# A transposing DMA for the attention operands, and three steps moved in the slots around it

## The reference

```
def expmap0(v): n = |v|;  return tanh(n) * v / n
def logmap0(x): n = |x|;  return arctanh(min(n, 1 - 1e-5)) * x / n
def plin(x, w, b): return expmap0(logmap0(x) @ w + b)
...
ada = t_emb @ w_ada + b_ada          # six rows of 256 for each sequence
xn = layer_norm(logmap0(x))
xm = expmap0(xn * (1 + sc_msa) + sh_msa)
q = _to_heads(plin(xm, w_q, b_q))    # 16 heads of 16; k and v alike
...
scores = einsum('bhqd,bhkd->bhqk', qt, kt) / sqrt(16)
attn = softmax(scores)
out_h = expmap0(einsum('bhqk,bhkd->bhqd', attn, vt))
attn_out = plin(_from_heads(out_h), w_o, b_o)
x = mobius_add(residual, expmap0(g_msa * logmap0(attn_out)))
...                                  # then an MLP half in the same manner
```

## Time and profile before

| | us |
|---|---|
| median of 3 runs | 839.33 (838.67 to 840.11) |
| the profiled execution | 841.73 |
| its span on the core | 839.9 |
| prologue, up to the first projection | 61.6 |
| attention half, first to last projection | 61.6 to 530.8 |

### The profile page before, as it was taken

One profiled execution on the slowest core, in us unless ns is written; L12 is line 12 of the kernel. 1 busy time (PEld: TensorE's weight loads), 2 busy tenths in 40 slices (PEclk: granted clock), 3 DMA queues, 4 the chain that ended last, 5 costly groups with the idle time before them and its releaser, 6 DMA issues.

```text
span 839.9 us, 29703 instructions
## 1 busy us (share of the span) xinstructions
PE 703.7 (84%) x9393; PEld 515.0 (61%) x9393; DVE 673.6 (80%) x2231; ACT 586.5 (70%) x1627; POOL 353.3 (42%) x682
## 2 busy tenths in 40 slices
PE   5967999999999999999999999731868899889986
PEld 2756777777777777777777777520325555556555
DVE  3868888888888888888888888757797888888885
ACT  1125777777777777777777777633577888888874
POOL 1005555556555565555555565401232333233231
PEclk9979999999999999999999999955899999999999
DMA  9931111111111111111111110021343545455432
GB/s 324 354 86 52 51 52 51 56 56 46 50 54 56 56 43 51 56 56 52 44 54 56 55 46 27 23 66 51 88 116 98 148 137 144 126 150 151 138 102 100
DMA packets 51811, 73.99 MB, mean 88 GB/s; under 512 B 7081, under 2 KB 34609, under 8 KB 51762
## 3 DMA queue, kind: packets, MB, share of 16 engines
q1 hardware_dynamic: 49970, 70.55, 28.4%
q10 hardware_dynamic: 1792, 2.89, 0.9%
HBM read 64.24 MB, written 9.18 MB: 87 GB/s over the span
## 4 chain that ended last, share of the span: by engine, by line
PE 44%; DVE 25%; issue 14%; DMA 5%; ACT 4%; SPq 3%; DVEq 2%; POOL 2%; POOLq 0%; ACTq 0%
PE p_qkv L893 21%; PE p_oz L867 8%; DVE u L1156 7%; PE p_s L958 3%; PE p_s L883 3%; DMA mod_b<-mod_rows 3%; SPq L365 2%; DVE g_all L1191 2%; PE p_qkv L958 2%; PE p_oz L861 2%; DMA x_all<-in_x 2%; DVEq L50 2%; PE p_t L944 1%; DVE qk L1231 1%; PE p_o L972 1%
## 5 line engine op out<-in xcount | busy, mean ns | idle before, releaser
L893 PE MATMUL p_qkv<-wqkv,tT 128*128 128x256 f32 x768 | 194.3, 390 | 26.6 <-DVE u L1156 26.3
L893 PEld LDWEIGHTS p_qkv<-wqkv,tT 128*128 128x128 f32 x768 | 135.1, 192 | 57.4 <-issue 23.8
L477 POOL TENSOR_TENSOR qk<-qk 128x512 f16<-128x512 f32 x64 | 73.9, 1155 | 142.0 <-ACT qk L613 142.0
L907 PEld LDWEIGHTS p_o<-v,pT 64*64 64x64 f32 x4096 | 68.3, 136 | 36.1 <-issue 36.1
L1184 DVE TENSOR_TENSOR z<-p_oz,bo 128x256 f32<-128x256 f32 x64 | 27.1, 424 | 77.5 <-PE p_oz L867 77.3
L618 ACT ACTIVATE qkT<-p_s 128x1024 f32<-128x1024 f32 x64 | 65.5, 1023 | 31.1 <-PE p_s L850 31.1
L907 PE MATMUL p_o<-v,pT 64*64 64x17 f32 x4096 | 72.8, 209 | 12.0 <-ACT pT L663 12.0
L663 ACT ACTIVATE pT<-p_s 128x1024 f32<-128x1024 f32 x64 | 65.4, 1022 | 20.3 <-PE p_s L883 20.3
L867 PE MATMUL p_oz<-wo,oT 128*128 128x256 f32 x256 | 75.2, 418 | 0.6 <-ACT oT L623 0.5
L850 PE MATMUL p_s<-ident,qk 128*128 128x128 f16 x1024 | 67.9, 219 | 6.7 <-issue 4.5
L1222 DVE TENSOR_TENSOR qk<-u,fac 128x256 f32<-128x256 f32 x128 | 70.3, 588 | 0.1
(11 more groups left out here) (268 smaller groups left out, 1758.0 us busy)
## 6 DMA issues: line engine op xcount, KB each, us to landing
mod<-mod_rows SPq DMA_DIRECT2D x128, 128.0 KB, 2.8
x_all<-in_x SPq DMA_DIRECT2D x8, 1024.0 KB, 13.9
gate<-mod_rows SPq DMA_DIRECT2D x128, 64.0 KB, 2.5
mod<-mod_rows SPq DMA_DIRECT2D x32, 256.0 KB, 4.1
mod_b<-mod_rows SPq DMA_DIRECT2D x32, 256.0 KB, 4.1
out<-x_all SPq DMA_DIRECT2D x32, 256.0 KB, 2.2
gate<-gate_rows SPq DMA_DIRECT2D x32, 128.0 KB, 3.5
bqkv<-gate_rows SPq DMA_DIRECT2D x32, 128.0 KB, 3.8
```

What stands on the lines that cost most here:

```text
L477: pool.tensor_tensor(low, qk[:, :].rearrange("p (a h d) -> p a h d", a=2, d=HD), qk4[:, :, :, 0, :], ALU.subtract).then_inc(low_ready, 1)
L893: mm = pe.matmul(p_qkv[:, a * D:a * D + D], tT[:, k, c, :], wqkv[:, c, a * D:a * D + D], start=c == 0, stop=c == C - 1)
L907: mm = pe.matmul(p_o[S * e:S * e + S, col:col + VW], pT[keys, e, g, :], v[keys, k, 2 * g + e, :], start=True, stop=True, skip_group_check= ...
```

## The change

The 16 matmul transposes and the copy out of PSUM are gone. In their place SP issues one DMA with transpose=True for each tile, from qk4 in SBUF to qkT in SBUF. qk4 gets a second buffer by parity (qk4s), which lies over mod_b, a tensor of the second half; bias_left, which had lain there, moves to xa. scores waits for the DMA's semaphore qkT_in instead of the copy's, and also for the exponential that last read p_s.

A new lag L_G = 7 holds gate_z, dot_x, the square of the gated z, and keep_stats; the sums st are double. So there is one slot more, 71 in place of 70. SP fetches the gate rows at lag 6 instead of 5. ScalarE makes the high parts ahead of the output copy evac_oT. GpSimd makes the low parts behind the token root. VectorE's order behind the row sums is gate, clip, dot, repeats, bias sum; it was bias sum, repeats, gate, clip, dot.

```diff
@@ sync
                 if on(h, off, L_H):
                     i, k = 2 * h + off - L_H, (off - L_H) % 2
+                    sp.wait_ge(again_ready, 2 * i + 2)
+                    after(sp, s_psum, i)
+                    sp.sem_inc(rows_begun, 1)
+                    sp.dma_start(qkT[:, :, :, :].rearrange("p a g n -> p (a g) n"),
+                                 qk4s[k].rearrange("p a h r d -> p (a h r d)"), transpose=True).then_inc(qkT_in, 16)
+                if on(h, off, L_L):
+                    i, k = 2 * h + off - L_L, (off - L_L) % 2
                     after(sp, zg_ready, i - 1)
                     for b in range(TB):
                         sp.dma_start(gate[S * b:S * b + S, k, :], mod_row(i, b, 2 * D, 3 * D)).then_inc(gate_in[k], 16)
@@ scalar
-            def high_parts(i):
+            def high_parts(i, k):
 
                 act.wait_ge(qk_ready, 2 * i + 2)
-                after(act, qkT_psum, i)
-                after(act, low_ready, i)
-                after(act, again_ready, 2 * i)
-                act.activation(qk4[:, :, :, 0, :], qk[:, :].rearrange("p (a h d) -> p a h d", a=2, d=HD), ACT.Copy).then_inc(high_ready, 1)
-
-            def evac_qkT(i):
-                act.wait_ge(qkT_psum, i + 1)
-                after(act, s_psum, i)
-                act.activation(qkT[:, :, :, :].rearrange("p a g n -> p (a g n)").bitcast(F32), p_s[:, :], ACT.Copy).then_inc(qkT_ready, 1)
+                after(act, qkT_in, 16 * (i - 1))
+                act.activation(qk4s[k][:, :, :, 0, :], qk[:, :].rearrange("p (a h d) -> p a h d", a=2, d=HD), ACT.Copy).then_inc(high_ready, 1)
@@ tensor
             def scores_wait(i):
 
-                pe.wait_ge(qkT_ready, i + 1)
+                pe.wait_ge(qkT_in, 16 * i + 16)
+                after(pe, p_ready, i)
...
-                if on(h, off, L_H):
-                    transpose_qk(2 * h + off - L_H)
```

More of the change, by code:

```diff
@@ L325, in run_tiles @@
         def run_tiles(eng, slot):
-            run_slots(eng, slot, FIRST, T, T + L_L)
+            run_slots(eng, slot, FIRST, T, T + L_G)
         def run_pairs(eng, slot):
@@ L469, in scale_v, with low_parts, keep_stats @@
                                    fac[:, 2 * H:3 * H].unsqueeze(2).broadcast_to([P, H, HD]), ALU.mult).then_inc(v_ready, 1)
-            def low_parts(i):
+            def low_parts(i, k):
                 pool.wait_ge(high_ready, i + 1)
                 pool.wait_ge(qk_ready, 2 * i + 2)
-                after(pool, qkT_psum, i)
-                low = bass.AP(qk4[:, :, :, :, :].tensor, 2 * HD, [[8 * H * HD, P], [4 * H * HD - HD, 2], [4 * HD, H], [1, HD]])
-                pool.tensor_tensor(low, qk[:, :].rearrange("p (a h d) -> p a h d", a=2, d=HD), qk4[:, :, :, 0, :],
+                after(pool, qkT_in, 16 * (i - 1))
+                big = qk4s[k]
+                low = bass.AP(big.tensor, big.offset + 2 * HD, [[8 * H * HD, P], [4 * H * HD - HD, 2], [4 * HD, H], [1, HD]])
+                pool.tensor_tensor(low, qk[:, :].rearrange("p (a h d) -> p a h d", a=2, d=HD), big[:, :, :, 0, :],
                                    ALU.subtract).then_inc(low_ready, 1)
-            def keep_stats(i):
+            def keep_stats(i, k):
                 pool.wait_ge(z_squared, i + 1)
@@ L648, in inverse_norms, with square_z, square_zg @@
                 act.activation(y0[:, :], lnh[:, :], ACT.Exp, scale=-0.5).then_inc(y0_ready, 1)
-            def square_z(i):
+            def square_z(i, k):
                 act.wait_ge(z_ready, i + 1)
-                after(act, stats_kept, i)
+                after(act, stats_kept, i - 1)
                 after(act, z_squared, i)
-                act.activation(junk[:, 1, :], z[:, :], ACT.Square, accum_out=st[:, 0:1]).then_inc(z_squared, 1)
+                act.activation(junk[:, 1, :], z[:, :], ACT.Square, accum_out=st[:, k, 0:1]).then_inc(z_squared, 1)
+            def square_zg(i, k):
                 act.wait_ge(zg_ready, i + 1)
@@ L834, in _ @@
             pe.wait_ge(rows_in, 64)
-            pe.wait_ge(ident16_made, 1)
             def transpose_t(i):
@@ L842, in transpose_t @@
                 mm.then_inc(tT_psum, 1)
-            def transpose_qk(i):
-                pe.wait_ge(again_ready, 2 * i + 2)
-                after(pe, p_ready, i)
-                for a in range(2):
-                    for g in range(G):
-                        mm = pe.transpose(p_qkT[:, a, g, :], qk4[:, a, 2 * g:2 * g + 2, :, :].rearrange("p h r d -> p (h r d)"),
-                                          ident16[:, :])
-                mm.then_inc(qkT_psum, 1)
             def output_waits(i):
@@ L1189, in gate_z, with dot_x @@
                 dve.wait_ge(gate_in[k], 32 * half + 32)
[L1190 removed]
+                after(dve, stats_kept, i - 1)
                 dve.scalar_tensor_tensor(out=tile_of(g_all, i), in0=z[:, :], scalar=1.0, in1=gate[:, k, :],
[L1192 to L1194 removed]
+                                         op0=ALU.mult, op1=ALU.mult, accum_out=st[:, k, 1:2]).then_inc(zg_ready, 1)
+            def dot_x(i, k):
                 dve.wait_ge(zg_ready, i + 1)
@@ L1223, in scale_qk, with repeat_parts @@
                                       fac[:, a * H:a * H + H].unsqueeze(2).broadcast_to([P, H, HD]), ALU.mult).then_inc(qk_ready, 1)
-            def repeat_parts(i):
+            def repeat_parts(i, k):
                 dve.wait_ge(high_ready, i + 1)
                 dve.wait_ge(low_ready, i + 1)
-                after(dve, qkT_psum, i)
-                q4, k4 = (qk4[:, a, :, :, :].rearrange("p h (y z) d -> p h y z d", y=2) for a in range(2))
+                after(dve, qkT_in, 16 * (i - 1))
+                q4, k4 = (qk4s[k][:, a, :, :, :].rearrange("p h (y z) d -> p h y z d", y=2) for a in range(2))
                 dve.tensor_copy(q4[:, :, :, 1, :], q4[:, :, :, 0, :]).then_inc(again_ready, 1)
```

59 lines of the change are left out of this document (28 added, 31 removed).

## The result

The changed kernel takes 851.01 us (median of 4 runs, 848.7 to 854.7), the kernel before, on the same chip, 839.72 (838.7 to 841.5). The ratio is 1.0136, with a 95% interval of 1.0091 to 1.0182: slower by 1.4%, or 11 us. The sign is the one forecast; the size is not: the forecast was 880 us, +41, and +11 were paid. The profiled execution has a span of 852.9 us, 13.0 more than the one of before. It is the slowest of the four (854.7 us), 3.7 above their median.

What follows compares the result with a forecast made beforehand. The prediction took circles of waits through VectorE's z-to-u work and GpSimd's roots as the bound. A slot of 8.16 us, 0.63 more, gave +37 us over 59 slots, plus +4 at the ends: +41, forecast 880 us, range 822 to 965.

Steps and rivals of the forecast that it cites:

- The bound before: In the 64-tile loop, a circle through VectorE's wait for z, 1.1 us a slot, and an equally late chain through GpSimd's roots.
- the two-slot circle: Loop path from repeats through DMA, scores, norms, roots, limit, gate and dot to repeats: L + 10.82 us for two slots.
- The slope of one half: In the loop, each microsecond of DMA landing above 4.24 us costs 0.5 us a slot, 29.5 us in 59 slots.
- L: Transposing DMA's time from issue to landing: 5.5 us, with 25 ns a piece as middle; 4.24 us would leave the slot unchanged.
- fixed part: In a DMA's landing, about 2.3 us that stand before the time for the bytes.
- rival 2: The transposing DMA lands like a plain one of the same bytes, 4.1 us: no change, 839 us; chance 0.07.
- Rival 3: Transposing DMA bound by its pieces or issue, SP or engines held 8 us or more: 973 us or worse; chance 0.15.
- rival 1: The transposing DMA lands within 4.1 us, so the loop gets faster: 803 us or 822 us; chance 0.25.
- The ends: Five more transposing DMAs before and behind the counted slots: +17 us if all were seen, taken as +4.
- GpSimd's low parts "at nothing": GpSimd's low parts, moved behind the token root, cost nothing, since GpSimd waits 2.3 us in each of 26 slots there.
- The floor of 6.4 us a slot: VectorE's own work in a loop slot, 7.53 - 1.1 us; reaching it would give back 65 us over 59 slots.
- Rival 4: TensorE's clock falls to 1.2 GHz as it is less busy: +0.7 us a slot, +41, 921 us; chance 0.08.

Runs made afterwards that it cites:

- dma_late: The changed kernel with the slot's two gate DMAs issued ahead of the transposing DMA instead of behind it: 913.37 us, ratio 1.0851.
- plain_copy: The changed kernel with a plain DMA of the same 512 KB instead of the transposing one, exponential's scale 1e-3 of its value, so another output: 832.68 us, ratio 0.9920.
- after_fill: The changed kernel with four extra fp32 identity transposes a slot on TensorE, read by nobody: 849.36 us, ratio 1.0093.
- rot_t: The changed kernel with VectorE's shift of t ahead of the square sums and its loop's branch moved behind the projection into u: 852.67 us, ratio 1.0124.
- no_dma: The changed kernel with the 16 matmul transposes and ScalarE's copy out of PSUM put back in place of the DMA, all other moves kept: 813.84 us, ratio 0.9704.
- nodma_rot_t: The changed kernel with matmul transposes and ScalarE's copy back, t ahead of the square sums, VectorE's branch moved behind the projection into u: 817.41 us, ratio 0.9704.

## Why the prediction was right in its sign and wrong in its size

Point by point, by its own steps.

**The bound before and the two-slot circle: right.** The wait for z vanished, and waits for qkT and for the roots came, where the prediction put them. With the measured landing the circle of its own terms is 10.82 + 4.2 = 15.02 us, the one read from the trace 15.12, and two slots in the loop take 7.34 + 7.83 = 15.17. The slope of one half was borne out by dma_late's pairs of slots at full clock.

**The step that failed is the size of L.** The prediction took the middle between 12.5 and 49 ns a piece, 25 ns, and so 3.2 us of transfer and L = 5.5 us. The count of pieces was right: the page of after has 184930 DMA packets where that of before has 51811, so 133119 more, 2080 for each of 64 tiles, against 2048 forecast. The sum of a full fixed part and the pieces' time was not. The plain copy landed in 3.1 us, where the fixed part of 2.3 us and the bytes' share alone, 1.6 us, give 3.9. For a piece, the DMA views of 200 to 400 us have 54606 packets more than before, and a share of 53.9% of 16 engines against 16.9%: an estimate of 22 ns each, near to the 25 taken. 130 of them are 2.8 us, and then only 1.4 us is left of the landing for all else. If the fixed part is kept at 2.3 us instead, a piece comes to 15 ns. No run separates the two; that their sum is 1.25 us too long is shown. The choice of the middle "in ratio" had no row behind it, and the prediction's own shortest estimate from its rows, 2.2 + 0.8 = 3.0 us, was right for a plain copy. The error in the loop is 59 x (5.5 - 4.25) / 2 = 37 us, which is more than the whole miss of 29 us (880 against 851).

**The number of rival 2 was near, and its reason was not.** It had 839 us, from a landing equal to a plain one's, put at 4.1 us. A plain one takes 3.1, and transposing 1.1 us more: two errors that cancel, so its number was near by luck. Half of 1.1 us, over 59 slots, is 32 us; plain_copy gave back 18 of it, probably because it ran into the clock.

**Rival 3: not borne out.** SP was held for 1.63 to 2.03 us by the issue, not for 8, and sixteen blocks landed in 4.2 to 4.3 us. In rival 1 the 822 us does not follow from its -19, which gives 820; it is the low end of the range, and the measured time is far from it.

**Loop, forecast against measured.** With L = 4.25 the prediction's sum gives +0.3 us in the loop and +4 at the ends, 844 us. The loop of the profiled execution had +8.2. Of the remaining 8 us the circle's other terms have 59 x (10.87 - 10.82) / 2 = 1.5 us (10.87 being the 15.12 less 4.25). The profiled after_fill takes 89.55 to 537.08 for the same slots, 447.5 us, which is 3.1 more than the kernel before and 5.1 less than the changed one. So 5.1 of the 8.2 us go when TensorE is kept busy: three of the changed kernel's slots, of 7.82, 7.82 and 9.72 us, have a granted clock of 0.78, 0.78 and 0.82, and its first four are longer too (7.85 on the mean, against 7.62). By the medians the two kernels differ by 1.7 us only, so 5.1 is an upper figure. About 1.3 us of the loop stays unexplained.

**The ends: +4 forecast, +4.8 in the trace.** The start took +3.4. The windows view of its last part reads:

```profile
60.00:100.00 40.00, 31.49 (x383) 23.55 (x381) 27.47 (x70) 19.30 (x49) 17.47 (x38) 0.83 0.40 84
```

The clock is 0.83, where the kernel before has 0.99. TensorE is idle for the DMA there (0.65 us at 76.37), and four matmuls behind that wait take 2.08 us, not 1.13. The four transposes of after_fill change little here: its clock is 0.89 in this stretch, and its first counted slot starts at 89.55. That the sum of the ends agrees is partly luck: the +4 was an allowance, and named no slot.

**GpSimd's low parts "at nothing": wrong in the reason, small in the sum.** The prediction asked only whether GpSimd has room, and it has. It did not ask which VectorE instruction would lie beside them. The shift of t went from 0.47 to 1.19 us. GpSimd's Newton steps went the other way (0.56 and 0.47 us beside VectorE's gate and dot, 0.29 and 0.28 now), and the two nearly cancel in the circle. In the floor they don't, but a short t alone did not lower it: in the order that makes it short, most of the gain goes to gaps between dependent instructions (rot_t).

**The floor of 6.4 us a slot: wrong.** "If nothing else came, 59 slots would give back 65 us." no_dma is the closest test, and gives 26. VectorE's stretched t takes 0.72 us of the 1.1 that its wait had left free, and with the 16 transposes still on it TensorE is at 96%. The floor is at 7.1 us, from VectorE in no_dma and from TensorE in nodma_rot_t.

**Rival 4, the clock: wrong as a price, right as a thing to watch.** In the changed kernel it is worth 2 to 5 us (the medians of after_fill and of the changed kernel differ by 1.7, their ratios by 0.0043, their profiled loops by 5.1). The waits of 0.6 us on the mean in every second slot left it at 1.00 in most of the loop. But as soon as the wait was moved and TensorE's slots became short and uneven, it cost 16 us.

**The chances.** Faster had 0.25, on account of a DMA of 4.1 us or less. It came at 4.25, 0.01 from the break-even of 4.24, and the sign was decided by what was costed at the ends and at nothing. That the sign came out as forecast is luck as far as L goes.

## What to carry to other kernels

Moving work from busy engines to a DMA sets a fixed time from issue to landing in the place of instruction time, and what it costs depends on where the wait for it stands in the waiting engine's order: here work of 1.1 us that didn't need the data stood behind it, and moving the wait took back 14 us. When a change has parts, time each alone: these were worth -26 and +37 us, and the kernel with the moves alone (813.8 us, ratio 0.970) is the version to keep. Before putting an instruction "in the free time" of GpSimd, look at what VectorE runs there, and before shortening work ahead of a loop's branch, look at whether that work was covering the branch, or a gap between two instructions that depend on each other.

## What the runs showed of the hardware that was not expected

- A transposing DMA of 512 KB from SBUF to SBUF landed in 4.2 to 4.3 us, a plain one in 3.1. SP was held for 1.63 to 2.03 us by the issue of the one and for 0.51 by that of the other; a pair of plain 64 KB issues had held it for 1.15.
- VectorE's shift of t, with two SBUF inputs, took 1.25 us beside a GpSimd instruction of 1.15 us and 0.47 us without it. A reduction with one input took 0.95 beside it and 0.94 alone.
- The clock of TensorE fell to the lower level for single groups of eight matmuls (3.43 us, 0.55 granted over 3.5 us), behind idle times of about 1 us, in loops whose clock over 100 us reads 0.95 to 0.97. Four extra transposes a slot, 0.6 us of work, brought 16 us in two such kernels.
- The branch of VectorE's loop cost 0.75 us when the instruction ahead of it was done in time, and nothing when one of 1.0 us ran over it.
- An instruction of VectorE that stood right behind the one whose result it reads waited 0.15 to 0.24 us for it (t behind lnx, rot_t). With an independent one in between, that gap was not seen.
